# Weights of a projection prepared inside the preceding stage's loop, and an attention stage entered engine by engine

## The reference

```
x = _layernorm(x + gated_linear_attention(x))      # 4 heads, chunks of 64
x = _layernorm(x + mixture_1(x))                   # layer norm, top 2 of 8 experts of width 768, a shared expert of 256
x = _layernorm(x + differential_attention(x))      # 16 heads of 2 x 16, rotated queries and keys, causal
x = _layernorm(x + mixture_2(x))                   # top 2 of 8 linear pairs 256 -> 256 -> 256
```

```
q = (x @ Wq.T + bq);  k = (x @ Wk.T + bk);  v = (x @ Wv.T + bv)
q1, q2, k1, k2 = rotated halves of each head (cos, sin of the position)
s1 = q1 . k1 / 4;  s2 = q2 . k2 / 4;  causal mask;  a = softmax(s1) - lam * softmax(s2)
out = rms_norm(a @ v) * head_norm_w @ Wo.T + bo
```

## Time and profile before

| | |
|---|---|
| median of 3 runs | 2619.53 us (2618.07 to 2623.4) |
| profiled execution | 2623.85 us, its span 2621.8 us |
| busy: PE / DVE / ACT / POOL | 2322.9 / 1585.8 / 1353.1 / 687.6 us |
| loop of the first mixture | about 567 to 1097 us |
| end of that stage to the first TT of `rope` | 1102.2 to 1132.7 us |
| loop of `rope` | 1132.7 to 1313.4 us |
| end of it to the first maximum of `attention` | 1313.4 to 1333.0 us |
| `attention` and second mixture | from there to the end |

### The profile page before, as it was taken

One profiled execution on the slowest core, in us unless ns is written; L12 is line 12 of the kernel. 1 busy time (PEld: TensorE's weight loads), 2 busy tenths in 40 slices (PEclk: granted clock), 3 DMA queues, 4 the chain that ended last, 5 costly groups with the idle time before them and its releaser, 6 DMA issues.

```text
span 2621.8 us, 49163 instructions
## 1 busy us (share of the span) xinstructions
PE 2322.9 (89%) x17112; PEld 1399.5 (53%) x17112; DVE 1585.8 (60%) x2625; ACT 1353.1 (52%) x2583; POOL 687.6 (26%) x754
## 2 busy tenths in 40 slices
PE   7999995989999999768749899899889898997998
PEld 5777774546666666556613333333343333336887
DVE  3566564633333333279867777777767777713788
ACT  5666662212333333233207888788768887884000
POOL 1222122003333333235622222322322232221000
PEclk9999996989999999979858999999999999988899
DMA  4223222652222222323320100010001000001000
GB/s 159 81 102 118 97 75 101 242 168 35 36 37 37 37 37 37 91 103 124 125 95 26 45 35 30 23 48 26 26 26 44 26 31 21 26 2 65 17 25 25
DMA packets 89352, 164.01 MB, mean 63 GB/s; under 512 B 15921, under 2 KB 63537, under 8 KB 87457
## 3 DMA queue, kind: packets, MB, share of 16 engines
q1 hardware_dynamic: 75488, 142.10, 15.5%
q0 software_dynamic: 13632, 18.77, 4.4%
HBM read 99.81 MB, written 60.49 MB: 61 GB/s over the span
## 4 chain that ended last, share of the span: by engine, by line
PE 37%; DVE 7%; ACT 6%; issue 5%; DMA 1%; SPq 1%; POOL 0%; ACTq 0%; DVEq 0%
PE PS L1985 10%; PE PS L2037 6%; PE PS L2009 5%; ACT E L1805 4%; PE PS L58 3%; PE PS L2004 3%; PE PS L59 3%; PE PS L60 3%; DVE NM L1903 2%; DVE TT L1438 2%; PE PS L1938 2%; PE PS L1961 1%; DVE PP L1401 1%; ACT OH L1840 1%; PE PS L2263 1%
## 5 line engine op out<-in xcount | busy, mean ns | idle before, releaser
L1903 DVE TENSOR_REDUCE NM<-PS 128x2 f32<-128x1024 f32 (+3 forms) x608 | 692.2, 1163 | 240.9 <-PE PS L2009 232.2
L1805 ACT ACTIVATE E<-PS,SCL 128x512 f32<-128x512 f32 (+2 forms) x1280 | 734.0, 650 | 187.9 <-PE PS L2037 184.2
L1985 PE MATMUL PS<-E,VP 128*32 128x256 f32 (+1 forms) x5120 | 381.7, 381 | 0.7 <-ACT OT L1833 0.7
L2037 PE MATMUL PS<-QS,KS 50*128 50x512 f16 (+3 forms) x1536 | 301.6, 335 | 38.5 <-ACT E L1805 37.5
L1736 POOL TENSOR_SCALAR_AFFINE_SELECT E<-E 128x512 f32<-128x512 f32 x256 | 162.9, 636 | 498.4 <-ACT E L1805 498.4
L1052 DVE SCALAR_TENSOR_TENSOR XIL<-PS,XSC,XIH 128x128 f16<-128x128 f32 x142 | 43.2, 346 | 347.0 <-ACT XIH L872 347.0
L2009 PE MATMUL PS<-KS,QS 48*128 48x512 f16 (+3 forms) x1536 | 241.9, 347 | 10.1 <-DVE NM L1903 9.5
L882 ACT ACTIVATE HB<-PS 128x768 f32<-128x768 f32 x71 | 57.6, 811 | 310.7 <-PE PS L1189 310.7
L1985 PEld LDWEIGHTS PS<-E,VP 128*32 128x32 f32 x5120 | 110.2, 110 | 167.2 <-issue 129.4
L2037 PEld LDWEIGHTS PS<-QS,KS 50*128 50x128 f16 x1536 | 112.7, 95 | 158.8 <-ACT E L1805 138.4
L1200 PE MATMUL PS<-WALL,HB 128*128 x852 | 195.7, 379 | 1.0 <-ACT HB L882 1.0
(11 more groups left out here) (334 smaller groups left out, 4063.0 us busy)
## 6 DMA issues: line engine op xcount, KB each, us to landing
parts<-PP SPq DMA_DIRECT2D x32, 512.0 KB, 2.9
WIN<-in_we SPq DMA_DIRECT2D x16, 768.0 KB, 5.0
WALL<-pairs_of_weights SPq DMA_DIRECT2D x7, 1536.0 KB, 7.2
QS<-parts SPq DMA_DIRECT2D x64, 128.0 KB
KS<-parts SPq DMA_DIRECT2D x64, 128.0 KB
pairs_of_weights<-WPH SPq DMA_DIRECT2D x16, 384.0 KB, 2.3
pairs_of_weights<-WPL SPq DMA_DIRECT2D x16, 384.0 KB, 3.2
WALL<-in_we SPq DMA_DIRECT2D x7, 768.0 KB, 8.5
```

The source lines that it names most:

```text
L1805: e.activation(dst, src, ACT.Exp, scale=K.SCL[:]).then_inc(S.ex, 1)
L1903: e.tensor_reduce(dst, src, AX, ALU.max).then_inc(S.mx, 1)
L1985: a = e.matmul(PS[32 * jj:32 * jj + 32, 7, 512 - n + c0:512 - n + c1], VP[b % 2][:, kt, 17 * hd:17 * hd + 32], E[:, m % NE, jj, c0:c1], st ...
L2037: a = e.matmul(PS[:, singles[i % 3], c:c + n], KS[w % 4][r, y, 128 * kt:128 * kt + 128], QS[w % 4][r, y, q0:q0 + n], start=True, stop=True)
```

## The change

1. **Room.** The room of NALL is used again: for `W`, the split weights, the raw weights with their squares, and the tables (`turned_weights`), later for E of `attention`, and for ZH of the last stage. QS and KS of the first three buffers (`K.QK`), the mask MRF, and IDB and MR are now kept from `rope` on. Half of the last stage's weights go into the room of `K.QK`, and its `choice` tiles into OT.
2. **Weights in the mixture's loop.** SP loads weights and biases as soon as the last transpose of the normed rows is done, and the tables after the low halves are made. ACT, DVE and PE do the preparation in tiles 4 to 18 of the loop, in the functions `prepare` and `row_lengths`. The two CS tables are scaled in four pieces. The wait for the sums' maxima moves into `turn_rows`.
3. **`rope` begins with X.** Only BB, WV, BV and X are loaded, all eight groups at once, then the mask. DVE sets the ones of VS first. ACT makes IDB and MR before the high half of WV.
4. **First fetches early.** SP issues the fetches of groups 0, 1 and 2, with the constant rows of KS, in blocks 12, 14 and 16 of `rope`.
5. **Entry one by one.** Into `attention`, PE waits for the last TT, the last values and the mask (`read`), DVE and GpSimd for the cleared bank alone, ACT for all of `rope` before its first exponential, SP as before. PE no longer waits for the mask in its first maximum.

```diff
 def moe(...), sp
+        e.wait_ge(S.pe_snt, 16)
+        for i in HALF:
+            e.dma_start(W.raw[i], A["wqk"][i]).then_inc(S.ww_ld, 16)
+            e.dma_start(BQK[:, i, :], A["bqk_all"][i]).then_inc(S.ww_ld, 16)
+        e.wait_ge(S.ww_lo, 2)
+        e.wait_ge(S.ww_sq, 2)
+        e.dma_start(W.tables[0][:], A["c_cs"]).then_inc(S.cs_ld, 16)
 act
+        def prepare(s):
+            if s == 4:
+                e.wait_ge(S.ww_ld, 64)
+                e.activation(BQK, BQK, ACT.Abs).then_inc(S.ww_ab, 1)
+            if s in (6, 7):
+                e.wait_ge(S.ww_mx, 1)
+                e.activation(W.squares[s - 6], W.raw[s - 6], ACT.Square).then_inc(S.ww_sq, 1)
+            if s in (8, 9):
+                e.activation(W.high[s - 8][:], W.raw[s - 8], ACT.Copy).then_inc(S.ww_hi, 1)
+            if s == 12:
+                e.wait_ge(S.ww_mx, 3)
+                n = own.act.on(e.activation(RW[:], MW[:], ACT.Ln, scale=256.0))
+                e.wait_ge(own.act.sem, n)
+                e.activation(RW[:], RW[:], ACT.Exp, scale=0.5).then_inc(S.ww_rt, 1)
+            if 15 <= s < 19:
+                i, k = int(s < 17), s % 2
...
+                e.activation(W.tables[i][:, k, :], W.tables[0][:, k, :], ACT.Copy, scale=CQ[:, i:i + 1]).then_inc(S.ww_cs, 1)
 dve
+        def prepare(s):
+            if s == 5:
+                e.wait_ge(S.ww_ab, 1)
+                e.tensor_reduce(MB[:], BQK, AX, ALU.max).then_inc(S.ww_mx, 1)
+            if s in (8, 9):
+                e.wait_ge(S.pe_ww, s - 7)
+                e.tensor_reduce(MW[:, s - 8:s - 7], PS[:, 6 + s % 2, :], AX, ALU.max).then_inc(S.ww_mx, 1)
+            if s in (10, 11):
...
+                e.tensor_tensor(W.low[s - 10][:], W.raw[s - 10], W.high[s - 10][:].bitcast(F32), ALU.subtract).then_inc(S.ww_lo, 1)
+            if s == 13:
...
 pe
+            if s in (10, 11):
+                e.wait_ge(S.ww_mx, s - 8)
...
+        def row_lengths(i, s):
+            e.wait_ge(S.ww_sq, i + 1)
+            for k in HALF:
+                a = e.matmul(PS[:, 6 + s % 2, :], ONE[:], W.squares[i][:, k, :], start=k == 0, stop=k == 1)
+            a.then_inc(S.pe_ww, 1)
...
+            if s in (8, 9):
+                row_lengths(s - 8, s)
 def rope(...), sp
         residual(0)
-        for i in HALF:
-            e.dma_start(WW[i], A["wqk"][i]).then_inc(S.r_ld_ww, 16)
-            e.dma_start(BQK[i], A["bqk_all"][i]).then_inc(S.r_ld_ww, 16)
-        for d, n in ((WV1, "wv1"), (BV, "bv"), (BB, "bqk"), (CS[0], "c_cs")):
+        for d, n in ((BB, "bqk"), (WV1, "wv1"), (BV, "bv")):
             e.dma_start(d[:], A[n]).then_inc(S.r_ld_v, 16)
-        for g in (1, 2, 3):
+        for g in range(1, 8):
             residual(g)
-        e.wait_ge(S.r_wwlo, 2)
-        e.wait_ge(S.pe_sqw, 2)
-        for g in (4, 5, 6, 7):
-            residual(g)
+        e.dma_start(K.MRF[:], A["c_mrc"]).then_inc(S.r_ld_mrc, 16)
...
+            if i in (12, 14, 16):
+                if i == 12:
+                    e.wait_ge(K.cleared, 2)
+                    for z, n in enumerate((3, 3, 2)):
+                        e.wait_ge(pp_st[z], 16 * n)
+                fetch_first(e, (i - 12) // 2)
 act
+        e.activation(K.IDB[:], K.IDN[:], ACT.Copy).then_inc(S.r_mrc, 1)
+        e.wait_ge(S.r_ld_mrc, 16)
+        e.activation(K.MR[:], K.MRF[:], ACT.Copy).then_inc(S.r_mrc, 1)
+    def read(e):
+        e.wait_ge(S.tt, 64)
+        e.wait_ge(S.r_val, 16)
+        e.wait_ge(S.r_mrc, 2)
 def attention(...)
     pool, dve
-        before.done(e)
+        e.wait_ge(K.cleared, 2)
     act
-        before.done(e)
+        e.wait_ge(K.cleared, 2)
...
                         elif i == 0:
-                            e.wait_ge(S.mr, 1)
+                            before.done(e)
     pe
-        before.done(e)
+        e.wait_ge(K.cleared, 2)
+        before.read(e)
```

More of the change, by code:

```diff
@@ L691, in choose_after, with choice, turned_weights @@
     top(C.M2, C.LG, C.R1)
[L694 to L695 removed]
+def choice(sb, tag, wide=None):
+    t = (wide or [sb(n + tag, [128, 32, 8])[:] for n in ("LG", "PB", "OH", "T8")]) + [sb(n + tag, [128, 32]) for n in ("M1", "M2", "R1")]
     return namedtuple("Choice", "LG PB OH T8 M1 M2 R1")(*t)
+def turned_weights(sb):
+    parts = [[sb(f"WW{n}{i}", [128, 2, 512], F32R) for i in HALF] for n in "HL"]
+    tables = [sb(f"CS{i}", [128, 2, 1024], F32) for i in HALF]
+    return namedtuple("Turned", "high low raw squares tables")(
+        parts[0], parts[1], [tables[0][:, :, 512 * i:512 * i + 512] for i in HALF], [tables[1][:, :, 512 * i:512 * i + 512] for i in HALF], tables)
+LARGEST = 2.0 ** 13
 MOE = group("""m_ld_cnt m_ld_shared m_ld_we m_xr0 m_xr1 m_st0 m_st1 m_one m_gex
     pe_snt pe_sup pe_sdn pe_cnt pe_xt pe_up0 pe_up pe_ht pe_dn
[L701 removed]
+    snt ssu shs sxa lgs probs chosen gap gexp pos te row gex rev gat hot pe_ss qs qr un gsc xsc xih wgt hots pe_idx half idx xit si hh ht yo
+    ww_ld ww_sq ww_ab ww_hi ww_lo pe_ww ww_mx ww_rt ww_cq cs_ld ww_cs""")
 def moe(nc, A, K, PS, D, own, before):
@@ L733, in moe @@
     C = choice(sb, "a")
+    W = K.W
+    BQK = W.squares[0]
+    MW, MB, RW, BD, CQ = (sb(n, [128, 2]) for n in ("MW", "MB", "RTW", "BD", "CQ"))
     t8 = lambda m: m.rearrange("p (t e) -> p t e", e=8)
@@ L1245, in rope @@
     NMR = sb("NMR", [128, 4])
-    WWH = [sb(f"WWH{i}", [128, 2, 512], F32R) for i in range(2)]
-    WWL = [sb(f"WWL{i}", [128, 2, 512], F32R) for i in range(2)]
+    W = K.W
+    WWH, WWL, CS = W.high, W.low, W.tables
     WV1, BV = sb("WV1", [128, 2, 256]), sb("BV", [128, 256])
@@ L1474, in bring @@
                     a.then_inc(S.pe_rx, 1)
-        for i in HALF:
-            e.wait_ge(S.r_sqw, i + 1)
-            e.wait_ge(S.r_ones, 1)
-            for k in HALF:
-                a = e.matmul(PS[:, 4 + i, :], ONES, SQW[i][:, k, :], start=k == 0, stop=k == 1)
-            a.then_inc(S.pe_sqw, 1)
         for n in range(BEFORE_K):
@@ L1667, in sp @@
         e.dma_start(LQ[:, 0:4, :], A["lam"]).then_inc(S.a_ld_lq, 16)
-        for i in range(4):
-            for x in HALF:
-                e.dma_start(KS[i][64 * x + 48:64 * x + 50, :, :], A["c_unit"]).then_inc(S.ones_k, 16)
-        fetch(1)
-        fetch(2)
+        unit_rows(e, 3)
         values(0)
@@ L2252, in join @@
                 for k in HALF:
-                    a = e.matmul(PS[:, bank, 256 * m:256 * m + 256], WI[:, x, k, 128 * m:128 * m + 128], WO2[:, x, k, :], start=k == 0, stop=k == 1)
+                    a = e.matmul(PS[:, bank, 256 * m:256 * m + 256], WI[x][:, k, 128 * m:128 * m + 128], WO2[x][:, k, :], start=k == 0, stop=k == 1)
             a.then_inc(S.pe_jn, 1)
@@ L2333, in _ @@
             def _(e):
-                for s in stages:
-                    s.sp(e)
+                st_gla.sp(e)
+                st_moe.sp(e)
+                st_rope.sp(e, parts.fetch_first)
+                st_att.sp(e)
+                st_mix.sp(e)
             @block.gpsimd
```

172 lines of the change are left out of this document (73 added, 99 removed).

## The result

The changed kernel took **2601.2 us** as a median of 4 runs (2593.12 to 2604.56), the kernel before 2621.47 us beside it (2618.07 to 2625.57): ratio 0.9918, 95% interval 0.989 to 0.9945, 20.3 us faster. Predicted were 2592 us, 27.3 us faster, with a range of 2585 to 2604. The profiled execution took 2593.12 us, its span is 2591.4. Measured twice more, each time beside the kernel before, it gave 0.9929 (0.9912 to 0.9945) and 0.9919 (0.9897 to 0.994).

The account below looks back on a forecast made before the run. PE bounds the mixture's loop, DVE the loop of rope and attention's first rounds, no engine the two seams; +3.4 +2.0 -13.6 +0.5 -19.6 = -27.3 us, from a median of 2619.53 to 2592 us, range 2585 to 2604.

Parts of the forecast that it names:

- four signs that it had named for being wrong: ACT idle for mask; DVE/ACT waits in rope blocks 13 to 18; gather 4 us later; first score under 19 us closer.
- The mixture's loop, +3.4: Mixture's loop: eight added row-sum matmuls on PE, which has no gap, lengthen it by 3.4 us; ACT's and DVE's additions stay hidden.
- Its start, +2.0: Before the mixture's loop: weight loads issued ahead delay the first gather; +2.0 us, the middle between 0 and 4.0.
- Entry into rope, -13.6: Seam before rope: weights already prepared, mask wait hidden by 1.8 us, first TT pair 13.6 us earlier; bounds -14 and -8.
- Rival 1: Seam into rope: gated by the loads, mask 5 us later, -8.6 in place of -13.6, 2597 us; chance 0.14.
- The loop of rope, +0.5: Loop of rope: fetches issued between stores fit into 11 us of slack; +0.5 us, bounds 0 and +5.
- rival 2: Loop of rope: fetches hold up the stores, three at 3 us each, +9 us, 2601 us; chance 0.10.
- Entry into attention, -19.6: Seam before attention: DVE takes its first maximum right after its last low part, 19.6 us earlier; bounds -20.9 and -17.

Follow-up runs that it names:

- experiment 8: Changed kernel with row sums, maxima, root, factors and table scaling moved out of the mixture's loop to behind it: 2590.81 us, ratio 0.9916.
- experiment 9: Changed kernel with spread fetches, bias in two pairs, sums behind the mixture's loop, mask ahead, weights' loads held until PE used gathered rows: 2590.11 us.
- experiment 10: Changed kernel with only the mask's load moved ahead of the seven other small loads of rope: 2595.89 us, ratio 0.9928.
- experiment 6: Changed kernel with the fetches of the first three groups issued two DMAs a block over blocks 12 to 26 of rope: 2594.74 us, ratio 0.992.
- experiment 5: Changed kernel with all engines entering attention together, as before, and the fetches still early: 2602.25 us, ratio 0.9955.
- experiment 3: Changed kernel with the fetches of groups 0 to 2 issued only when SP enters attention, engines still entering one by one: 2606.88 us, ratio 0.9961.
- experiment 7: Changed kernel with GpSimd's four large bias additions in two pairs, the low rows of group 0 between them: 2596.4 us, ratio 0.9924.

## Why the prediction came out as it did

The time lies in the range, and in the main the forecast's mechanism held: both seams got shorter, by about the sizes given. It was 7 us too good in the difference (27.3 for 20.3) and 9 in the time, as the kernel before took 2 us more beside it. Three of the four signs that it had named for being wrong showed all the same, each worth a few us: ACT stood idle for the mask's DMA, ACT waited for a store in blocks 17 and 19 of `rope` and DVE for PP in block 19, and the first score came only 17.0 us closer to the end of that loop (15.7 and 15.8 in the later traces), not 19. That the sum of the terms comes as near as it does is partly luck: +2.0 for a later start was not there, and +2.7 before the first score was in no term. By its steps:

- **The mixture's loop, +3.4.** Measured +3.5 in the first pair of traces, +3.7 in the last. Right, and experiment 8 takes 2.7 to 2.8 of it back by taking the sums away. Tile 12 cost nothing: the copies to HB stand at 660.60, 667.95 and 675.30 us, 7.35 apart on either side of it, though its three table loads took 1283 ns each. The Trainium skill, "ScalarE: Activation LUTs", What ACT_TABLE_LOAD costs, adds a drain of some 1380 ns to each; the trace shows the operation after a load 1.29 us behind its start (663.55 to 664.84) and no drain.
- **Its start, +2.0.** PE was idle 9.87 us before the gathered rows, against 9.04; in the later traces it was 8.95 before, and 8.62 and 8.46 after. The gather itself, from its issue to PE's use of it, took 6.11 and 6.05 us before and 6.01, 5.97 and 6.25 after, though the first loads of weights were issued ahead of it. With the loads held back (experiment 9) it took 5.87. So the term is 0 within 0.4, the lower bound; the middle between the bounds was the wrong choice here. The 5.5 us by which the first stage was shorter in the profiled pair are no effect of the change: the later traces put it at 565.7 and 565.4 us.
- **Entry into rope, -13.6.** Measured -13.1; -14.6 in the last pair, past the bound of -14. Right in size by two errors that cancel. The mask was not hidden: it released ACT 16.0 us after the stage's first load (1100.18), where 14.1 had been worked out, and so set the first TT. And PE was faster than assumed, since it stood at the lower clock for its first six matmuls only, and the first TT needs just six (in experiment 10 it starts at 1115.88, and the sixth ends at 1115.84). Rival 1 was right in its mechanism and wrong in its price of 5 us: with the mask ahead (experiment 10) the first TT comes 2.4 us earlier, and 0.9 us of that are left at the end of the loop.
- **The loop of rope, +0.5.** Measured +1.9 in the profiled pair, +3.7 in the last. This step was mis-sized, and rival 2 is what happened, at a fifth to two fifths of its price. SP's time was counted nearly right (6.3 to 7.1 us a batch, for 5.6), but the slack of 11 us for a store assumed a landing in 2.9 us. Beside the fetches the stores landed after 9.1 us as a median between 1200 and 1262 us and after 14.0 at most, and ACT stood 7.5 us for a buffer. Experiment 6 shows the cause by taking it away. The row for it was there: a fetch took 14.9 us to land.
- **Entry into attention, -19.6.** Measured -19.7, with DVE's gap gone. Right in size. The early fetches alone close 15.2 us of it (experiment 5 leaves a gap of 4.4), and the entry one by one the last 4.5; without the early fetches it closes nothing (experiment 3). What is left of these 4.5 us at the first score is 1.0 to 1.8, by the next step.
- **What no step had: +2.7** before the first score, 3.5 in the other traces. Moving DVE 33 us ahead while GpSimd's additions moved 26 (1332.93 to 1306.77) made the two meet. This term was put at nothing. The prediction worked out that the additions would end late and asked who needs GpSimd's results, and that part held: the scores did not wait for the low rows. It did not ask which DVE instruction would run beside them. Experiment 7 shows the cause by taking the meeting away.

From the mixture's loop to the first score the table's stages sum to 810.0 us as a mean of two traces before, and to 786.2 as a mean of three after: -23.9 us. The medians saved 20.3, 17.7 and 22.4. So 1.5 to 6.2 us are missing. The first stage was not longer (566.9 us as a mean, 564.5 after); the rest behind the first score was, 1242.1 us before and 1245.5 after, though its work is the same. That stretch varies between 1240.6 and 1250.7 us over the ten traces with early fetches; summed over windows of 5 us, what the granted clock lacks of full speed between 1390 us and the end comes to 41.1 us in the shortest and 51.3 in the longest of them, so a good part of that scatter goes with the clock. The clock does not explain the 3.4 us between the two means, though: summed in the same way from the first score to the end, it lacks 56.5 and 52.3 us before, and 54.6, 58.7 and 51.7 after, nearly the same on average. Whether the change itself makes this stretch a little longer or two traces before are too few was not settled.

## What to carry to other kernels

When an engine is let ahead of the others, go through what will run beside it at its new place, and not only through what it needs and who needs it. Loads that are pulled ahead go in small portions between the transfers that others wait for; what matters is the landing of those transfers, not the time to issue the new ones. After moving a wait, read the time to the end of the stage, and know how far that end moves by itself: in experiment 10 the first landmark came 2.4 us earlier and the stage's end 0.9, while the length of this loop differed by 2.0 us between two traces of the kernel before.

## What the runs showed of the hardware

DVE's small combination, an operation on two inputs in SBUF with its output in SBUF, did not end while GpSimd worked through a row of additions in SBUF, whatever the size of one: 2.92 to 3.90 us in six traces with four additions of 2048 elements, and 7.74 us with 32 of 256 elements, in place of 0.17. DVE's maxima, which read PSUM, ran beside the same additions without delay (14.47 us for 13 of them, and 14.47 for the 13 of the next round, with no additions beside them). The Trainium skill, "SBUF — State Buffer", SBUF: two separate sides, says that DVE and GpSimd share a pair of ports, and that of a DVE operation with two inputs in SBUF and a GpSimd one that reads SBUF whichever starts first holds it for the whole instruction. The four large additions agree with that, as the last of them alone is 4.5 us long and had begun when the combination started. The 32 small ones do not, since a hold of one instruction would have ended within 0.7 us.

The mask's load took 9.87 us from its issue behind seven loads of X of 512 KB; between 1106 and 1116 us the DMA was at 313 GB/s and a share of 0.86, so this one stood behind real traffic. The stores of 512 KB did not: between 1200 and 1262 us they landed after 9.1 us as a median beside three batches of fetches, at 147 GB/s and a share of 0.41, and after 3.0 us with the fetches spread out, at 143 GB/s and 0.43. So how the transfers follow one another in the queue made them late, and not how much was moved.
